# Style product and turns of q and k in halves of 64 tokens on the two row halves of TensorE's array

## What is computed

```python
def attn(h):                                # h: 128 x 32 x 512
    qkv = clip(einsum('bsd,ed->bse', h, w_qkv), -8, 8)
    q, k, v = split(qkv, 3)
    q, k = layer_norm(q, q_ln_w, q_ln_b), layer_norm(k, k_ln_w, k_ln_b)   # over all 512
    scores = q @ k.T * 16 ** -0.5 + alibi, causal      # 32 heads of 16
    return einsum('bsd,ed->bse', softmax(scores) @ v, w_out)

h = einsum('bct,bcd->bdt', x, style_weights[style])    # 32 x 32 per batch: the style product
x = x + attn(h)
y = einsum('bsi,boi->bso', x, lora_weight[adapter])    # 512 x 512 per batch
x = x + layernorm(relu(y @ up) ** 2 @ down + (y @ fc1 @ expert) * gate(y) @ fc2)
```

## Time and profile before

| | |
|---|---|
| median of 3 runs | 1126.23 us (1125.78 to 1127.97) |
| the profiled execution | 1126.27 us |
| its span, first to last instruction | 1124.5 us |
| busy in the span: TensorE, its weight loads, VectorE, ScalarE, GpSimd | 97%, 79%, 60%, 54%, 63% |
| matmul records | 10996 |
| mean granted TensorE clock | 0.994 of full speed |
| mean DMA rate | 143 GB/s |

### The profile page before, as it was taken

How to read it: one execution, slowest core, us unless ns; L and a number is a source line. 1 busy time by engine, 2 the same in 40 slices (tenths; PEclk the granted TensorE clock), 3 DMA queues, 4 the chain that set the end, 5 groups by cost and what they waited for, 6 DMA issues and landing times.

```text
span 1124.5 us, 27403 instructions
## 1 busy us (share of the span) xinstructions
PE 1088.2 (97%) x10996; PEld 890.1 (79%) x10996; DVE 676.1 (60%) x1040; ACT 602.5 (54%) x985; POOL 713.4 (63%) x612
## 2 busy tenths in 40 slices
PE   5999999999999999999999999999999999999994
PEld 3878788888888888888877778787878888787883
DVE  5567666666666667667666245565655565554432
ACT  4466767676767677777776425335161625333220
POOL 4566888788888887878676464556455464533342
PEclk9999999999999999999999999999999999999997
DMA  7125555646464646565567953233514123030101
GB/s 277 41 79 182 171 201 166 202 160 212 158 209 158 214 152 219 172 211 156 201 226 234 375 166 95 85 96 106 113 48 133 59 90 99 29 85 29 47 29 37
DMA packets 95292, 160.77 MB, mean 143 GB/s; under 512 B 46400, under 2 KB 47168, under 8 KB 89792
## 3 DMA queue, kind: packets, MB, share of 16 engines
q1 hardware_dynamic: 79456, 118.16, 32.6%
q0 software_dynamic: 12224, 34.10, 9.5%
q10 hardware_dynamic: 3488, 6.78, 1.7%
HBM read 93.97 MB, written 42.47 MB: 121 GB/s over the span
## 4 chain that ended last, share of the span: by engine, by line
PE 95%; DMA 1%; issue 1%; DVE 1%; POOL 0%; ACT 0%; SPq 0%; DVEq 0%; ACTq 0%; POOLq 0%
PE bank L648 24%; PE pair L832 15%; PE bank L808 15%; PE bank L738 10%; PE bank L688 8%; PE bank L825 8%; PE pair L665 3%; PE bank L696 3%; PE pair L710 3%; PE bank L638 3%; PE bank L723 1%; PE bank L778 1%; PE bank L676 1%; DMA xt<-in_x,tile_rows 1%; PE bank L759 0%
## 5 line engine op out<-in xcount | busy, mean ns | idle before, releaser
L1675 POOL TENSOR_TENSOR w_lo<-w2t,w_hi 128x2048 fp32r<-128x2048 f32 x38 | 174.8, 4600 | 39.6 <-ACT w_hi L994 36.2
L648 PE MATMUL bank<-wqkv_hi,h_hi 128*128 128x512 f32 x384 | 153.9, 401 | 0.2
L648 PE MATMUL bank<-wqkv_hi,h_lo 128*128 128x512 f32 x384 | 150.0, 391 | 0.0
L648 PE MATMUL bank<-wqkv_lo,h_hi 128*128 128x512 f32 x384 | 149.7, 390 | 0.0
L1745 POOL TENSOR_TENSOR u_lo<-act,u_hi 128x512 fp32r<-128x512 f32 x64 | 82.7, 1292 | 103.3 <-ACT u_hi L1187 103.2
L808 PE MATMUL bank<-yT_hi,up_hi 128*128 128x512 f32 x256 | 100.8, 394 | 0.0
L808 PE MATMUL bank<-yT_hi,up_lo 128*128 128x512 f32 x256 | 99.8, 390 | 0.0
L1524 DVE TENSOR_TENSOR act<-act 128x512 f32<-128x512 f32 x59 | 67.0, 1135 | 54.6 <-ACT act L1183 54.6
L808 PE MATMUL bank<-yT_lo,up_hi 128*128 128x512 f32 x256 | 99.6, 389 | 0.0
L832 PE MATMUL pair<-down_hi,u_hi 128*128 128x512 f32 x256 | 99.6, 389 | 0.0
L832 PE MATMUL pair<-down_lo,u_hi 128*128 128x512 f32 x256 | 99.6, 389 | 0.0
(11 more groups left out here) (178 smaller groups left out, 2908.8 us busy)
## 6 DMA issues: line engine op xcount, KB each, us to landing
w2t<-in_w SPq DMA_DIRECT2D x38, 1024.0 KB
vx<-v_hl SPq DMA_DIRECT2D x128, 68.0 KB
x1g<-x_rows SPq DMA_DIRECT2D x32, 256.0 KB, 3.0
kx<-k_hl SPq DMA_DIRECT2D x124, 64.0 KB
x_rows<-x1t SPq DMA_DIRECT2D x31, 256.0 KB
ffn_high<-w_high SPq DMA_DIRECT2D x20, 256.0 KB, 3.6
ffn_low<-w_low SPq DMA_DIRECT2D x20, 256.0 KB, 3.3
stage<-in_wqkv SPq DMA_DIRECT2D x3, 1024.0 KB, 9.4
```

What stands on the lines that cost most here:

```text
L648: m = e.matmul(into, a[:, c, :], b[:, n, c, :], start=(c == 0 and k == 0), stop=(c == KC - 1 and k == 2))
L1675: e.tensor_tensor(w2_lo[:, :, :], w2t[:, :, :], w2_hi[:, :, :].bitcast(F32), ALU.subtract).then_inc(d_wlo, 1)
```

## The change

- The style product and the turns of q and k are made in two halves of 64 tokens. Per chunk there are two instructions in place of one: half g reads partitions 64g to 64g+63 of the data (64 rows by 128 features, stationary) and streams 64 columns of `style_bd` or of the identity. Each half stands on its own 64 rows of the array and writes its own PSUM bank.
- `style_bd` only has two blocks side by side (64 columns) instead of four; its mask shrinks with it.
- PSUM is laid out anew. Two pairs of banks are tensors of their own, `banks45` and `banks67`; h takes the first 256 columns of both banks of a pair, q the first and k the last 256 columns. B3 holds k's projection, the turned values and the output projection (tiles up to 27 and 28; B6 and B7 for the last ones), B4 v's projection, B5 the weight chunk, B2 also the turned slot, B3 route chunks 1 to 3.
- The waits follow the new owners: turns wait until the low parts of q and k of the tile before are made, style waits for v's clip (`cv`) and the weight chunk's low part, k's projection for the final add (`x1`) of tile i-5 and for the copies of route chunks, the scaling of q for both turns, the low part of q for both high parts.
- Order: for i < 4 style i+1 goes from before q's projection to between q's and k's, the route chunk from there to before q's. In the last steps ScalarE scales and rounds k and q of a tile together.

The core of the diff (the same edits of call sites left out):

```diff
-    own = p[:, None] // SEQ == np.arange(BPT)[None, :]
+    own = p[:, None] // SEQ % ROW_TILES == np.arange(ROW_TILES)[None, :]
...
-    bank = [psum(f"bank{i}", [P, DM]) for i in range(2, 8)]
+    B2, B3 = (psum(f"bank{i}", [P, DM])[:, :] for i in (2, 3))
+    banks45, banks67 = psum("banks45", [P, 2, DM]), psum("banks67", [P, 2, DM])
     pair = psum("pair", [P, 2, DM])
-    B2, B3, B4, B5, B6, B7 = (b[:, :] for b in bank)
+    B4, B5, B6, B7 = banks45[:, 0, :], banks45[:, 1, :], banks67[:, 0, :], banks67[:, 1, :]
...
-    def k_bank(t):
-        return B4 if t < 3 else B5
+    def half(banks, n):
+        return banks[:, :, n * KC * HALF:(n + 1) * KC * HALF].rearrange("p g (c t) -> p g c t", c=KC)
+    def by_half(tile):
+        return tile.rearrange("p c (g t) -> p g c t", g=ROW_TILES)
+    def h_banks(t):
+        return half(banks67 if t < 2 else banks45, 0)
+    def q_banks(t):
+        return half(banks67 if t < T - 1 else banks45, 0)
+    def k_banks(t):
+        return half(banks67 if t < T - 1 else banks45, 1)
+    def value_bank(t):
+        return B3 if t <= T - 5 else B6
+    def out_bank(t):
+        return B3 if t <= T - 4 else B7
...
-                upto(e, "x1", t - 6)
                 upto(e, "hlo", t - 1)
+                if t >= 2:
+                    upto(e, "cv", t - 1 if t > SHORT else t - 2)
+                if t > 5:
+                    e.wait_ge(r_low, min(t - 5, CHUNKS))
                 for c in range(KC):
-                    m = e.matmul(B6[:, P * c:P * c + P], xt[t % XR][:, P * c:P * c + P],
-                                 style_bd[t % 2][:, :, :].rearrange("p j d -> p (j d)"), start=True, stop=True)
+                    for g in range(ROW_TILES):
+                        rows = slice(HALF * g, HALF * g + HALF)
+                        m = e.matmul(h_banks(t)[:, g, c, :], xt[t % XR][rows, P * c:P * c + P],
+                                     style_bd[t % 2][rows, 0:ROW_TILES, :].rearrange("p j d -> p (j d)"),
+                                     start=True, stop=True)
...
                 for c in range(KC):
-                    m = e.transpose(into[:, P * c:P * c + P], src[:, P * c:P * c + P], ident)
+                    for g in range(ROW_TILES):
+                        rows = slice(HALF * g, HALF * g + HALF)
+                        m = e.transpose(into[:, g, c, :], src[rows, P * c:P * c + P], ident[rows, rows])
...
             def project_k(i):
                 upto(e, "ck", i - 1)
-                upto(e, "qhi", i - 2)
-                upto(e, "qlo", i - 2)
+                if 2 <= i <= KC:
+                    e.wait_ge(s_routec, i)
+                upto(e, "x1", i - 5)
                 project(i, 1, B3, "pk")
...
                 upto(e, "cv", i - 1)
-                upto(e, "khi", i - 2)
-                upto(e, "klo", i - 2)
-                project(i, 2, B5, "pv")
+                if 0 < i < SHORT:
+                    upto(e, "hlo", i + 1)
+                project(i, 2, B4, "pv")
...
+            def banks_free(t):
+                if t == T - 1:
+                    upto(e, "cv", T - 1)
+                    upto(e, "hlo", T - 1)
+                    e.wait_ge(r_low, CHUNKS)
+                elif t:
+                    upto(e, "qlo", t - 1)
+                    upto(e, "klo", t - 1)
+                else:
+                    upto(e, "hlo", 1)
...
             for i in range(T - 1):
-                if 0 < i < SHORT:
-                    style(i + 1)
-                project_q(i)
-                if i == 0:
-                    style(1)
                 if i in (2, 3, 4):
                     make_route(i - 1)
+                project_q(i)
+                if i < SHORT:
+                    style(i + 1)
                 project_k(i)
                 project_v(i)
...
             slot_in(LAST, B2)
             high_o(T - 5)
-            scale_k(T - 2, B5)
-            high_k(T - 2, B5, k_hl)
+            scale_k(T - 2)
+            scale_q(T - 2)
+            high_k(T - 2, k_hl)
+            high_q(T - 2)
             high_v(T - 1)
             normalize(T - 1)
-            scale_q(T - 2, B3)
-            high_q(T - 2, B3)
             soft_exp(T - 3)
-            scale_k(T - 1, B5)
-            high_k(T - 1, B5, k_last)
+            scale_k(T - 1)
+            scale_q(T - 1)
+            high_k(T - 1, k_last)
+            high_q(T - 1)
             high_o(T - 4)
...
-                e.tensor_tensor(style_bd[t % 2][:, :, :],
+                e.tensor_tensor(style_bd[t % 2][:, 0:ROW_TILES, :],
                                 style_rows[t % XR][:, :].rearrange("p (o d) -> p o d", o=1)
-                                .broadcast_to([P, BPT, SEQ]),
-                                cst[:, C_WMASK:C_ROW].rearrange("p (j d) -> p j d", j=BPT), ALU.mult) \
+                                .broadcast_to([P, ROW_TILES, SEQ]),
+                                cst[:, C_WMASK:C_ROW].rearrange("p (j d) -> p j d", j=ROW_TILES), ALU.mult) \
                     .then_inc(A["style"], 1)
```

More of the change, by code:

```diff
@@ L67 @@
 EARLY_GROUPS = 2
+ROW_TILES, HALF = 2, P // 2
 CLIP = 8.0
@@ L408, in slot_at @@
         return (1, 3) if m else (5, 6)
-    def k_bank(t):
-        return B4 if t < 3 else B5
+    def half(banks, n):
[12 more added lines that the diff above has]
+        return B3 if t <= T - 4 else B7
     def route_bank(c):
-        return pair[:, 0, :] if c == 0 else B7
+        return pair[:, 0, :] if c == 0 else B3
     def last_slot(m):
@@ L687, in out_project @@
                     for k, (a, b) in enumerate(((o_hi, wo_hi), (o_hi, wo_lo), (o_lo, wo_hi))):
-                        m = e.matmul(B6, a[:, j, :], b[:, j, :], start=(j == 0 and k == 0),
+                        m = e.matmul(out_bank(t), a[:, j, :], b[:, j, :], start=(j == 0 and k == 0),
                                      stop=(j == BPT - 1 and k == 2))
@@ L755, in make_route @@
                 e.wait_ge(s_fc2, 16)
-                if c >= 2:
-                    e.wait_ge(s_routec, c)
+                if c:
+                    upto(e, "ck", c)
                 for k in range(LC):
@@ L774, in gate_products @@
                     e.wait_ge(S["gc"], m)
+                else:
+                    upto(e, "qlo", T - 1)
+                    upto(e, "klo", T - 1)
                 for c in range(KC):
@@ L850, in _ @@
                          start=True, stop=True)
-            e.matmul(B7[0:1, 0:SLOTS], idc[:, :], onehot[:, 0::BPT], start=True, stop=True) \
+            e.matmul(B5[0:1, SLOTS:2 * SLOTS], idc[:, :], onehot[:, 0::BPT], start=True, stop=True) \
                 .then_inc(s_tp, 1)
@@ L934, in _ @@
             scores(T - 1)
+            upto(e, "x1", T - 4)
             up(0, 1)
@@ L962, in _ @@
                             e.wait_ge(S["route"], GROUP * m)
-                        else:
-                            upto(e, "qhi", T - 1)
-                            upto(e, "qlo", T - 1)
                         adapt_slot(slot_up(m), B7)
@@ L1141, in _ @@
             for i in range(T - 1):
+                if i in (2, 3, 4):
+                    keep_route(i - 1)
                 if i < SHORT:
@@ L1169, in _ @@
                 if i >= 1:
-                    scale_q(i - 1, B3)
-                    scale_k(i - 1, k_bank(i - 1))
-                    high_q(i - 1, B3)
-                    high_k(i - 1, k_bank(i - 1), k_hl)
+                    scale_q(i - 1)
+                    scale_k(i - 1)
+                    high_q(i - 1)
+                    high_k(i - 1, k_hl)
                 if i >= LAG:
@@ L1331, in low_k @@
                     upto(e, "kx", t - 1)
-                e.tensor_tensor(dst[:, 1, :], at, dst[:, 0, :], ALU.subtract).then_inc(A["klo"], 1)
+                parts = [by_half(dst[:, n, :].rearrange("p (c t) -> p c t", c=KC)) for n in range(2)]
+                e.tensor_tensor(parts[1], k_banks(t), parts[0], ALU.subtract).then_inc(A["klo"], 1)
             def divide(t):
@@ L1349, in add_x @@
                     e.wait_ge(a_store[t % 2], 16 * (t // 2))
-                e.tensor_tensor(x1t[t % 2][:, :], B6, xt[t % XR][:, :], ALU.add).then_inc(A["x1"], 1)
+                e.tensor_tensor(x1t[t % 2][:, :], out_bank(t), xt[t % XR][:, :], ALU.add).then_inc(A["x1"], 1)
             def low_planes(j):
@@ L1454, in _ @@
             step(e.tensor_scalar(table_f[2][:, :], B5[:, 0:SLOTS], ABSENT, pmod, ALU.add, ALU.add))
-            step(e.tensor_copy(table_f[3][0:1, :], B7[0:1, 0:SLOTS]))
+            step(e.tensor_copy(table_f[3][0:1, :], B5[0:1, SLOTS:2 * SLOTS]))
             step(e.tensor_copy(slot_rows[:, :], table_f[2][:, :]))
@@ L1476, in take_v @@
                 upto(e, "vlo", t - 2)
-                clip(t, B5, vf[t % 2][:, :], "cv")
+                clip(t, B4, vf[t % 2][:, :], "cv")
             def aggregate(t):
@@ L1535, in _ @@
             take_v(T - 1)
-            low_slot(LAST, B7)
+            low_slot(LAST, B2)
             low_o(T - 5)
-            low_k(T - 2, B5, k_hl)
```

(3 more changed lines are left out.)

105 lines of the change are left out of this document (49 added, 56 removed).

## The result

The changed kernel takes 1132.85 us (7 runs, 1130.5 to 1135.38) beside 1127.67 us for the kernel before in the same comparison: ratio 1.0052, interval 1.0036 to 1.0068: 5.2 us slower by the medians, 5.9 by the ratio. Measured again beside the last experiments it was 1130.88 against 1126.82, 1.0036 (1.0023 to 1.0049). Forecast were 4.7 us less. Its profiled execution, the slowest of the seven, took 1135.38 us with a span of 1133.6, against 1126.27 and 1124.5.

What follows compares the result with a forecast made beforehand. TensorE's stream was taken as the bound (97% busy). Loop tiles -7.5, styles alone +1.4, turns alone -1.1, waits +1.0 and +1.5, GpSimd 0: -4.7 us, from 1126.3 to 1121.6 us; range 1108 to 1132.

Steps and rivals of the forecast that it cites:

- by the round: Turns and style: two half matmuls at once; turns 0.061 us per round, -0.38 per tile; style 0.11, only -0.05.
- A gain per tile: Loop steps 4 to 30: -0.28 us per tile, counted 27 times as -7.5 us of the run.
- change of the piece size: New switch of array piece ahead of q's turn: TensorE stands 0.09 us, first load exposed 0.06; +0.15 per tile.

## What to carry to other kernels

Splitting small matmuls onto row halves paid by the round for the turns and not for the style product, almost only where neighbours shared the piece size (2.07 beside 2.26 us), and it doubles their instructions: count the instructions of each dense stretch beside its microseconds. A gain per tile is worth its sum only if every engine that feeds the stream has that margin in its worst tile, not on average. At the ends of the loop, where the order differs, follow every engine's queue, and count both kernels from an event that they share: an instruction that is 4 us later may have lost all of it earlier, and a wait of 3.1 us, as VectorE's here, may hold up next to nothing.

## What was not expected of the hardware

TensorE's instructions arrive in packets of 16 KB for 256 of them, and where these pass in about 2.6 us, TensorE may stand 1 to 2.7 us; 34 stands ended 2.2 to 2.8 us after a packet's start, and the stands move with the packet boundaries. A change of the piece size cost 0.09 us of standing and up to 0.10 for the first load behind it. In or behind stands and waits of 1.4 to 4.5 us, though not behind all, TensorE ran at 1.2 GHz for 3.4 us or twice that. The kernel before probably has it too in some runs, though not in its profile: of 28, the 15 with a mean clock of 0.993 have a median of 1127.9 us and the 8 with 0.995 one of 1125.4.
